# A fused attention and mixture-of-experts layer on one core: the weight-splitting steps at other places of a timetable

## The chip, the cores and the metric

The kernel runs on one core of a Trainium2 chip. The metric is the device time of one execution in microseconds; the time of a kernel is the median of its runs. The engines are TensorE (PE in the rows, PEld for its weight loads), VectorE (DVE), ScalarE (ACT), GpSimd (POOL) and SyncE (SP), which only issues DMAs. Each engine works through its own instructions in order, and waits on semaphores at the head of its queue.

## The reference

Eight sequences of 512 tokens with 256 features go through a pre-norm attention layer with 16 causal heads, then through a pre-norm layer of 8 experts, of which each token uses the 2 with the highest gate probability.

```python
x = x + attention(layernorm(x), W_qkv, b_qkv, W_out, b_out)      # 16 heads of 16, causal softmax
# second part, E = 8, H = 1024, TOP_K = 2
xn = (x' - mu) * rsqrt(var + 1e-5) * gamma + beta                 # x' = layernorm(x)
probs = softmax(xn @ gate_w); w, idx = top_k(probs, 2); w = w / w.sum()
h = gelu(einsum('bld,edh->eblh', xn, w1) + b1)                    # exact gelu
out_e = einsum('eblh,ehd->ebld', h, w2) + b2
x = x + sum over the two chosen experts of w * out_e + x'
```

## The kernel before

The program has three stages in the time of the core. First the projections of q, k and v (to 121 us). Then the attention, in 32 units (`UNITS`) of one batch and four heads each, which ends at about 508 us. Last the experts' matrix products over gathered tiles of 256 or 128 tokens, from 518 us on.

**The timetable.** From the attention on, nothing in the code says directly in which order an engine works. A table `table_of` maps a tick, a plain integer, to steps; `at(tick, stage, n)` adds one. Sorted by tick (and within a tick by the order in which the steps were added) it is one list, and every engine runs through it and does the part of each step that belongs to it. A tick is no time: it only orders. One unit has `UNIT = 48` ticks, so unit u lies from 48u on, and four units (192 ticks) are a batch.

**Per unit.** Five `combo` steps at 48u + 2, 11, 20, 30, 39: PE makes the transposed scores of unit u (L658) into three PSUM banks in turn, and the plain scores of a unit that comes 11 slots later (L630, L643); ACT takes the exponentials (L907, and L904 in the fifth combo), which frees the banks; DVE takes the row maxima of the later scores (L1240, L1242 with L1243, L1237). `load_unit` u + 3 at 48u - 4 makes SP issue eight DMAs with the q and k of a later unit (L1816, L1818); it waits until PE has made all scores of unit u - 1. `copy_o` (L927) copies the weighed values out. `keep_o`, `move_o`, `keep_inverse`, `move_inverse` (L1835, L1846, L1848, L1855, L1864) are SP's transfers of the results of earlier units through memory.

**Per batch.** The output projection and the second norm: `out_proj` and `gate` on PE (L716, L717 and L733), `load_again` on SP (L1890, the batch's x once more), `add_out` on DVE (L1260, which waits for it), `gamma` and `beta` on GpSimd for batches below 6 (L1756, L1759), `row_high` on ACT (L950), which waits for SP's `acc_out` (L1986) to have landed, and `rows_out` (L1978).

**Splitting the experts' weights.** The experts' products run in float16, with each weight as a high and a low part. 32 pieces of 128x1024 values (`W_SPLITS`) are split during the attention. Piece i takes these steps, in which `raw` is the piece in float32:

- `load_raw` i on SP (L1874), a DMA of 512 KB into the buffer for raw pieces. It waits until the piece that was in this buffer before has been split (`w_low`).
- `high_weights` i on ACT (L980): the float16 high part.
- `low_weights` i on DVE (L1402): the rest, from the raw piece and the high part. It waits for the high part.
- `store_weights` i on SP (L1882), for the first six pieces (`LENT = 6`) only. Their place in SBUF is still lent to the attention, so both parts are stored to memory with two DMAs and come back after it.

The first six pieces use one raw buffer and one pair of buffers for the parts:

```python
# load_raw, i < 6: the raw buffer of the piece before
w.wait_ge(sem("w_low"), raw_before[i] + 1)
# high_weights on ACT and low_weights on DVE, 0 < i < 6: all stores so far have landed
w.wait_ge(sem("w_stored"), 32 * i)
# store_weights
w.wait_ge(sem("w_low"), i + 1)
```

Pieces 6 to 31 use two raw buffers in turn, and write straight to the weights' place.

In the text behind this, high(i), low(i), raw(i) and store(i) are these four steps of piece i, and (u, c) is combo c of unit u.

Of the kernel before, what the change touches and what calls it, by code (L numbers as in the profile page):

```python
# [61 lines left out]
def build(nc, t):  # L62
# [54 lines left out]
    with ctx:  # L117
# [80 lines left out]
        LENT = -(-(HG * PT_LEN + V_LEN) // HALF)  # L198
# [87 lines left out]
        W_SPLITS = len(splits)  # L286
# [16 lines left out]
        UNIT = 48  # L303
# [13 lines left out]
        def at(tick, stage, n):  # L317
            table_of.setdefault(tick, []).append((stage, n))

        for u in range(UNITS):  # L320
            base = u * UNIT
# [39 lines left out]
        at(8 * 36 + 94, "spread_tops", 0)  # L361
        at(8 * 36 + 126, "find_scales_2", 0)

        split_ticks = [426 + UNIT * i for i in range(LENT)]
        split_ticks += [718 + 26 * i for i in range(W_SPLITS - LENT)]
        for i, base in enumerate(split_ticks):
            at(base - (24 if i < LENT else 35), "load_raw", i)
            at(base, "high_weights", i)
            at(base + 9, "low_weights", i)
            if i < LENT:  # L370
                at(base + 15, "store_weights", i)
# [7 lines left out]
        for b in range(B):  # L379
            base = (b + 1) * NG * UNIT  # L380
# [45 lines left out]
        for i, (batches, _, _, _) in enumerate(PARTS):  # L426

            base = max(ranked_at[batches - 1] + 16, 7 * NG * UNIT + 88) + (168 if i > ALL else 0)
# [11 lines left out]
        for j in range(-1, TILES):  # L440
            base = over + 58 + TILE_TICKS * j
# [1577 lines left out]
```

## Time and profile before

| | |
|---|---|
| median of 3 runs | 939.74 us |
| lowest, highest | 935.47, 952.23 us |
| the profiled execution: its own time | 935.47 us |
| its span, first to last instruction | 933.7 us |
| PE busy | 828.8 us, 89% of the span |
| DVE, ACT, POOL busy | 697.3, 572.1, 466.5 us |
| mean granted TensorE clock | 0.945 |

The profiled execution is the fastest of the three runs. Its time is 1.8 us longer than its span. The busy time of a stage is to be read beside the length of the stage: PE is nearly full in the experts' stage, and shares the attention with DVE and ACT.

### The profile page before, as it was taken

To read this page: it belongs to the slowest core of one execution; us is meant where nothing else is said; L and a number is where in the kernel's file an instruction comes from. 1 tells how busy PE (TensorE), PEld (TensorE's weight loads), DVE (VectorE), ACT (ScalarE), POOL (GpSimd) and SP (SyncE) were. 2 spreads that over 40 slices of the span, in tenths; PEclk is the share of its full clock that TensorE was granted. 3 is DMA by queue.
4 is the path that set the end of the run, shared out by engine and by line. 5 is a ranking of instruction groups with operands and counts; after the bars stand their busy time and mean duration, and the time that the engine had idled before them with its cause. 6 is when DMAs were issued, how large, how long until landed. Compare 5 with 4: busy or idle time off the path is not lost.

```text
span 933.7 us, 21008 instructions
## 1 busy us (share of the span) xinstructions
PE 828.8 (89%) x6760; PEld 551.7 (59%) x6760; DVE 697.3 (75%) x1566; ACT 572.1 (61%) x1048; POOL 466.5 (50%) x575
## 2 busy tenths in 40 slices
PE   4899988887888879887977799989999999999996
PEld 3555522332433324342424698868888888888875
DVE  6777889778689897979795587866676756666654
ACT  1867566657868787978686474544544444454543
POOL 4100023333635847767577548783577555455432
PEclk9999988889999988898899799999999999999999
DMA  9888758755777676577827884453436453444341
GB/s 210 257 281 269 250 174 239 207 130 172 230 199 221 185 196 183 166 212 183 218 75 248 151 140 78 78 116 65 81 62 92 74 82 70 84 72 80 49 70 24
DMA packets 185047, 139.40 MB, mean 149 GB/s; under 512 B 98064, under 2 KB 167568, under 8 KB 184816
## 3 DMA queue, kind: packets, MB, share of 16 engines
q1 hardware_dynamic: 153444, 95.16, 39.8%
q0 software_dynamic: 15776, 18.95, 13.0%
q10 hardware_dynamic: 15724, 23.95, 7.9%
q8 instruction: 61, 1.00, 0.5%
q14 instruction: 42, 0.34, 0.1%
HBM read 83.63 MB, written 44.80 MB: 138 GB/s over the span
## 4 chain that ended last, share of the span: by engine, by line
PE 54%; DVE 16%; DMA 13%; SPq 6%; issue 4%; POOL 3%; ACT 3%; POOLq 0%; ACTq 0%
PE banks L777 18%; PE banks L795 17%; PE banks L599 5%; DMA arena<-qk_parts 3%; DVE arena L1240 3%; PE banks L716 3%; PE banks L702 2%; PE banks L589 2%; DVE weights L1402 2%; PE banks L658 2%; DVE arena L1242 2%; DMA out<-arena 2%; DMA arena<-arena 2%; DMA arena<-token_rows,arena 2%; SPq L1816 2%
## 5 line engine op out<-in xcount | busy, mean ns | idle before, releaser
L996 ACT ACTIVATE arena<-banks,arena 128x256 f32<-128x256 f32 (+1 forms) x312 | 152.8, 542 | 188.8 <-PE banks L777 98.0
L777 PE MATMUL banks<-arena,weights 128*128 128x256 f16 (+1 forms) x1872 | 207.8, 268 | 12.7 <-DMA arena<-arena 11.9
L777 PEld LDWEIGHTS banks<-arena,weights 128*128 x1872 | 175.8, 99 | 39.4 <-issue 14.6
L795 PE MATMUL banks<-weights,arena 128*128 x1704 | 193.9, 273 | 0.8 <-DVE arena L1532 0.7
L1739 POOL DMA_INDIRECT out<-arena x71 | 115.0, 1620 | 145.5 <-DVE arena L1543 98.5
L795 PEld LDWEIGHTS banks<-weights,arena 128*128 128x128 f16 x1704 | 165.2, 98 | 22.4 <-issue 1.7
L658 PE MATMUL banks<-arena 64*128 64x128 f16 (+3 forms) x512 | 119.4, 326 | 17.8 <-ACT arena L907 5.5
L1530 DVE TENSOR_SCALAR arena<-arena 128x512 f16<-128x512 f32 (+1 forms) x156 | 75.2, 482 | 77.9 <-ACT arena L996 76.1
L630 PE MATMUL banks<-arena 62*128 62x384 f16 (+3 forms) x512 | 92.7, 324 | 32.6 <-DVE arena L1237 9.0
L1532 DVE SCALAR_TENSOR_TENSOR arena<-arena 128x512 f16<-128x512 f32 (+1 forms) x156 | 110.2, 706 | 5.6
L658 PEld LDWEIGHTS banks<-arena 64*128 64x128 f16 x512 | 38.4, 99 | 99.0 <-ACT weights L907 26.3
L1240 DVE TENSOR_REDUCE arena<-banks 128x2 f32<-128x1024 f32 x64 | 77.9, 1217 | 20.5 <-PE banks L643 20.0
L907 ACT ACTIVATE arena<-banks,arena 128x512 f32<-128x512 f32 x128 | 81.8, 686 | 18.3 <-PE banks L658 17.6
L907 ACT ACTIVATE weights<-banks,arena 128x512 f32<-128x512 f32 x128 | 80.3, 684 | 11.1 <-PE banks L658 10.6
L1715 POOL DMA_INDIRECT arena<-token_rows,arena x71 | 76.2, 1073 | 20.2 <-issue 18.0
L1686 POOL DMA_INDIRECT slot_tokens<-arena x64 | 68.0, 1062 | 21.6 <-issue 17.0
L1242 DVE TENSOR_REDUCE arena<-banks 128x2 f32<-128x768 f32 x64 | 60.9, 951 | 20.5 <-PE banks L643 20.2
L1700 POOL TENSOR_SCALAR_AFFINE_SELECT weights<-weights 128x512 f32<-128x512 f32 (+1 forms) x80 | 45.0, 580 | 60.2 <-ACT weights L907 55.3
L1700 POOL TENSOR_SCALAR_AFFINE_SELECT arena<-arena 128x512 f32<-128x512 f32 (+1 forms) x80 | 47.5, 610 | 39.4 <-ACT arena L907 37.8
L1543 DVE SCALAR_TENSOR_TENSOR arena<-banks,arena 128x256 f32<-128x256 f32 x71 | 31.4, 480 | 44.6 <-PE banks L795 41.4
L702 PE MATMUL banks<-arena 128*32 128x256 f32 (+3 forms) x512 | 57.1, 525 | 6.1 <-ACT arena L927 2.3
L630 PEld LDWEIGHTS banks<-arena 62*128 62x128 f16 x512 | 28.7, 98 | 54.8 <-DVE arena L1237 13.3
(199 smaller groups left out, 1273.9 us busy)
## 6 DMA issues: line engine op xcount, KB each, us to landing
weights<-in_L_ffn_w ACTq DMA_DIRECT2D x16, 1024.0 KB, 8.8
arena<-in_L_ffn_w SPq DMA_DIRECT2D x32, 512.0 KB
qk_parts<-weights SPq DMA_DIRECT2D x64, 128.0 KB
arena<-qk_parts SPq DMA_DIRECT2D x128, 64.0 KB, 3.4
weighed_values<-arena SPq DMA_DIRECT2D x32, 256.0 KB
token_rows<-arena SPq DMA_DIRECT2D x12, 512.0 KB, 4.3
arena<-qk_parts SPq DMA_DIRECT2D x128, 32.0 KB, 3.5
arena<-weighed_values SPq DMA_DIRECT2D x32, 128.0 KB
```

The costliest lines, as they stand in the source:

```text
L630: pe.matmul(bank[:, to:to + (qt + 1) * P], q_st[u % 4][half, h, qt * P:qt * P + P], k_st[u % 4][half, h, 0:(qt + 1) * P], start=(to == 0), ...
L658: m = pe.matmul(turn_bank(number)[:, to:to + T - kt * P], k_st[u % 4][half, h, kt * P:kt * P + P], q_st[u % 4][half, h, kt * P:T], start=T ...
L777: m = pe.matmul(bank[:, c * TILE:c * TILE + WIDTH[j]], w1[:, k, wp, f:f + P], xp[:, k, 0:WIDTH[j]], start=(i == 0), stop=(i == len(terms) ...
L795: m = pe.matmul(bank[:, c * D:(c + 1) * D], hp[:, f, c * P:(c + 1) * P], w2[:, f // (FC // 2), wp, f % (FC // 2), :], start=(f == 0 and i ...
L907: act.activation(p_T[u % 2][:, PAIR * h + j, PT_AT[kt]:PT_AT[kt] + T], bank, ACT.Exp, scale=EXP_SCALE).then_inc(sem("exped"), 1)
L996: m = act.activation(h_32[r % 2][:, c, 0:WIDTH[j]], banks[:, 1 + c2, c * TILE:c * TILE + WIDTH[j]], ACT.Gelu, bias=b1_now[j % 2][:, 2 * c2 ...
L1240: m = v.tensor_reduce(out[:, :, slot // 2, 3], pair, AX.X, ALU.max, negate=True)
L1242: v.tensor_reduce(out[:, :, slot // 2, 2], pair[:, :, 0:3 * P], AX.X, ALU.max, negate=True)
L1532: v.scalar_tensor_tensor(h_low[:, pair, width], h_32[r % 2][:, :, width], SCALE_H, h_high[:, pair, width], ALU.mult, ALU.subtract).then_in ...
L1700: m = g.affine_select(out=area, in_=area, compare_op=ALU.is_ge, fill=0.0, base=0, pattern=pattern, channel_multiplier=-1)
L1715: g.indirect_dma_start(gathered[j % 3][:, c, :], None, rows_dram[:, :], bass.IndirectOffsetOnAxis(slot_of(j, c), 0)).then_inc(sem(f"gather ...
L1739: g.indirect_dma_start(acc_dram[:, :], bass.IndirectOffsetOnAxis(slot_of(j, c), 0), y[j % 2][:, c, :], None, compute_op=ALU.add).then_inc( ...
```

## The change

Two numbers of the timetable are changed for the first six pieces, and one for the others. The steps of piece i < 6 stand 42 ticks apart and no longer 48, from the same first tick. Their `load_raw` stands 30 ticks ahead of `high_weights` and no longer 24. Pieces 6 to 31 stand 24 ticks earlier, with the same distance of 26 ticks.

```diff
-        split_ticks = [426 + UNIT * i for i in range(LENT)]
-        split_ticks += [718 + 26 * i for i in range(W_SPLITS - LENT)]
+        split_ticks = [426 + 42 * i for i in range(LENT)]
+        split_ticks += [694 + 26 * i for i in range(W_SPLITS - LENT)]
         for i, base in enumerate(split_ticks):
-            at(base - (24 if i < LENT else 35), "load_raw", i)
+            at(base - (30 if i < LENT else 35), "load_raw", i)
             at(base, "high_weights", i)
             at(base + 9, "low_weights", i)
             if i < LENT:
                 at(base + 15, "store_weights", i)
```

The instructions of PE and POOL keep their order. Those of ACT, DVE and SP change places.

On ACT, in unit 11 (L932 is a copy of the batch's turned rows, L960 and L966 copies of the output projection and the gate). Before:

```order
L907 ACTIVATE arena<-banks,arena 128x512 x2
L932 COPY arena<-banks 128x512
L907 ACTIVATE arena<-banks,arena 128x512 x4
L904 ACTIVATE arena<-banks,arena 128x2x256 x2
L927 COPY arena<-banks 128x512
L980 ACTIVATE arena<-arena 128x1024
L960 COPY arena<-banks 128x512
L966 COPY arena<-banks 128x32
```

Now:

```order
L907 ACTIVATE arena<-banks,arena 128x512 x2
L932 COPY arena<-banks 128x512
L907 ACTIVATE arena<-banks,arena 128x512 x2
L980 ACTIVATE arena<-arena 128x1024
L907 ACTIVATE arena<-banks,arena 128x512 x2
L904 ACTIVATE arena<-banks,arena 128x2x256 x2
L927 COPY arena<-banks 128x512
L960 COPY arena<-banks 128x512
```

high(3) moved from behind the copy that ends the unit to a place between the exponentials of (11, 2) and of (11, 3).

On SP, around the eight loads of unit 14, of which the last stands first here. Before:

```order
L1818 DMA arena<-qk_parts 16x2x512
L1835 DMA weighed_values<-arena 128x512
L1864 DMA arena<-inverse_sums 64x1x512
L1827 DMA arena<-v_rows 128x4x64
L1882 DMA late_weights<-arena 128x1024 x2
L1855 DMA inverse_sums<-arena 128x16
L1920 DMA arena<-arena 2x8x128 x2
L1874 DMA arena<-in_L_ffn_w 128x4x256
```

Now, from the row ahead of the eight loads on (six of them are left out):

```order
L1848 DMA arena<-weighed_values 128x1x16
L1986 DMA out<-arena 128x4x256
L1874 DMA arena<-in_L_ffn_w 128x4x256
L1816 DMA arena<-qk_parts 32x2x512
...
L1818 DMA arena<-qk_parts 16x2x512
L1882 DMA late_weights<-arena 128x1024 x2
L1835 DMA weighed_values<-arena 128x512
```

raw(3) moved from behind the eight loads to the place ahead of them, where it waits for low(2), and store(2) now follows them at once.

On SP, at `load_again` of batch 4. Before:

```order
L1978 DMA token_rows<-arena 128x4x256
L1874 DMA arena<-in_L_ffn_w 128x1024
L1846 DMA arena<-weighed_values 64x1x512
L1848 DMA arena<-weighed_values 128x1x16
L1890 DMA arena<-in_L_attn_x 128x4x256
```

Now:

```order
L1978 DMA token_rows<-arena 128x4x256
L1846 DMA arena<-weighed_values 64x1x512
L1848 DMA arena<-weighed_values 128x1x16
L1890 DMA arena<-in_L_attn_x 128x4x256
L1874 DMA arena<-in_L_ffn_w 128x4x256
```

The load of a raw piece moved from ahead of `load_again` to behind it.

## Rows read from the trace of the kernel before

**Rows 1.** Busy by stretch: length, PE, PEld, DVE, ACT, POOL, PEclk, DMA share, GB/s

```profile
212.00:256.00 44.00, 35.97 (x305) 15.54 (x301) 35.00 (x65) 34.70 (x60) 24.12 (x37) 0.92 0.67 207
256.00:300.00 44.00, 37.43 (x324) 15.57 (x321) 38.67 (x80) 35.60 (x64) 18.51 (x29) 0.92 0.73 204
300.00:475.00 175.00, 148.97 (x1209) 68.21 (x1207) 151.54 (x281) 139.04 (x238) 118.67 (x158) 0.90 0.70 189
```

**Rows 2.** The 26 later high parts by source line: durations, first and last start

```profile
L980 ACT ACTIVATE weights<-arena x26: 1130/1147/1171, 291.8 to 469.6; 128x1024 f16<-128x1024 f32 x26
```

**Rows 3.** Timeline of DVE, in unit 10

```profile
242.02 1.23 DVE L1240 TENSOR_REDUCE arena<-banks 128x2 f32<-128x1024 f32 x1
```

**Rows 4.** The low parts of the first six pieces by source line

```profile
L1402 DVE SCALAR_TENSOR_TENSOR arena<-arena x6: 1276/1277/2209, 223.9 to 283.1; 128x1024 f16<-128x1024 f32 x6
```

**Rows 5.** Timeline of SP's queue, units 10 and 11

```profile
241.81 0.33 SPq L1816 DMA_DIRECT2D arena<-qk_parts  x1
...
244.99 0.43 SPq L1818 DMA_DIRECT2D arena<-qk_parts  x1
...
247.57 0.98 SPq L1882 DMA_DIRECT2D late_weights<-arena  x2
...
250.60 0.40 SPq L1874 DMA_DIRECT2D arena<-in_L_ffn_w  x1
```

**Rows 6.** The stores of the first six pieces, issue to landing

```profile
DMA to landing us min/median/max: 2.0/3.2/4.5
```

**Rows 7.** Timeline of ACT, unit 11: start, length, idle time before

```profile
248.58 1.24 ACT L907 ACTIVATE arena<-banks,arena 128x512 f32<-128x512 f32 x2
250.15 1.27 ACT L907 ACTIVATE arena<-banks,arena 128x512 f32<-128x512 f32 x2 [0.32 <-PE banks L658]
...
254.68 1.15 ACT L980 ACTIVATE arena<-arena 128x1024 f16<-128x1024 f32 x1 [1.32 <-DMA arena<-in_L_ffn_w]
```

**Rows 8.** Timeline of PE, from the last combo of unit 11

```profile
251.43 0.38 PE L658 MATMUL banks<-arena 64*128 64x256 f16 x2
...
251.86 1.08 PE L716 MATMUL banks<-arena 128*128 128x256 f32 x4
...
253.87 1.85 PE L733 MATMUL banks<-arena 128*128 128x8 f32 x16
```

**Rows 9.** Chain of waits, 205 to 300 us: start, length, what

```profile
283.18 2.13 DVE arena L1402
285.33 0.33 SPq L1882
...
295.44 5.36 DMA arena<-qk_parts
```

**Rows 10.** Timeline of GpSimd, 336 to 341 us

```profile
336.79 2.36 POOL L1759 TENSOR_TENSOR arena<-arena 128x1024 f32<-128x1024 f32 x1
```

**Rows 11.** Timeline of DVE, the same stretch

```profile
335.90 1.16 DVE L1240 TENSOR_REDUCE arena<-banks 128x2 f32<-128x1024 f32 x1
336.98 3.25 DVE L1402 SCALAR_TENSOR_TENSOR weights<-arena,weights 128x1024 f16<-128x1024 f32 x1
```

**Rows 12.** Chain of waits, 390 to 436 us

```profile
403.83 1.67 SPq L1874
...
406.76 8.14 DMA arena<-in_L_attn_x
...
414.92 0.69 DVE arena L1260
```

**Rows 13.** Chain of waits, 440 to 520 us, the end of the attention

```profile
473.35 1.19 DVE weights L1402
...
492.59 5.74 DMA arena<-inverse_sums
...
510.70 7.45 DMA arena<-arena
```

**Rows 14.** Timeline of DVE: the first step that needs all low parts

```profile
484.76 0.16 DVE L1419 TENSOR_SCALAR arena<-arena 128x8 f32<-128x8 f16 x1
```

## The prediction

> **What bounds the kernel now.** I first read the busy time by stretch, since the change lies between 212 and 475 us only. In the long stretch from 300 to 475 us, 175 us, PE is busy for 149.0, DVE for 151.5 and ACT for 139.0 [rows 1]. No engine is the bound alone: each is at 79 to 87%, and each waits for the next in turn. PE cannot start a score before ACT has freed a bank, ACT cannot take exponentials before PE has made the score, and DVE's maxima free the banks of the plain scores. From 212 to 300 us PE is at 82 and 85%, DVE at 80 and 88% [rows 1]. So work that is moved within this part is neither free nor paid in full. What counts is whether it stands on the chain at its place. The number of steps is the same in both kernels, 32 high and 32 low parts.
>
> For a tick's size I take the high parts of pieces 6 to 31. Between ticks 718 and 1368 they start from 291.8 to 469.6 us [rows 2]: 177.8 us for 650 ticks, 0.274 us each.
>
> **The change part by part.** The last 26 pieces stand 24 ticks earlier and 26 apart. So piece i + 1 stands now 2 ticks behind the place that piece i had. Nearly the whole train of steps keeps its surroundings with the number shifted by one. What is left is this: one piece more is split before tick 728, none is split at 1368 to 1377, and some steps jump over a neighbour that stands within 2 ticks. The first six need a look each. I find five places that move time.
>
> (a) The store of piece 2 lands late, a cost. raw(3) now stands at tick 522, ahead of the eight loads of unit 14, and waits for low(2) at 519. On DVE low(2) follows the maxima of (10, 4), which end at 242.02 + 1.23 = 243.25 [rows 3]; it takes 1.28 [rows 4], to 244.53. SP then issues raw(3) in 0.40 [rows 5], to 244.95 with the gap, and the eight loads, which took 244.99 + 0.43 - 241.81 = 3.61 [rows 5], to 248.56. Only then come the two stores of piece 2, 0.98 [rows 5], to 249.54, the second of them issued at about 249.05. A store lands 3.2 us after its issue, at least 2.0, at most 4.5 [rows 6]: at 252.25 (251.05 to 253.55). high(3) stands now right behind the exponentials of (11, 2), which end at 248.58 + 1.24 = 249.82 [rows 7], and waits for this landing: 2.4 us (1.2 to 3.7). ACT is in order, so the exponentials of (11, 3) stand behind it: high(3) takes 1.15 [rows 7], one exponential about 0.65 (half of 1.27 for two), and the bank that PE needs for the last score of (11, 4) is free at 252.25 + 1.15 + 0.65 = 254.05. PE made it at 251.43 [rows 8]. That is 2.6 later (1.4 to 3.9). PE goes from there through the output projection and the gate without a pause, to 253.87 + 1.85 = 255.72 [rows 8], and so passes the delay on in full. The old wait of high(3) for its raw piece, 1.32 [rows 7], gives nothing back, since PE was busy with that projection over it. The loads of unit 14 also go out 3.2 later (245.0 for 241.8), but their first use is the fifth combo of unit 11, which this same wait puts off. **+2.6 us (+1.4 to +3.9).**
>
> [...]
>
> (b) low(5) leaves the place where it collided, a gain. The chain of waits runs through low(5) from 283.18, 2.13 long, then through SP's store(5), and on to the loads of unit 18, whose landing PE awaits [rows 9]. It is the one of the first six that took 2.21 where the others took 1.28 [rows 4]. Now it stands 30 ticks earlier, and low(6) comes in at tick 703, ahead of the same loads: 2.13 out and 1.28 in, with SP's raw(8) waiting for it as store(5) did. **-0.9 (-2.1 to 0;** the first end if low(6) falls into a wait for PE**).**
>
> (c) In batch 2 GpSimd's beta step, L1759, runs from 336.79 to 339.15 [rows 10]. A low part that starts at 336.98 takes 3.25 and not 1.28 [rows 11]: it does not run until GpSimd is done, and then takes its own time. The reduction ahead of it, which reads PSUM, took 1.16 with its head in the same stretch [rows 11]. The low part that now stands here, at tick 885 for 883, is behind the maxima of tick 884. These run while GpSimd does, and the low part ends at 340.2 as before. About 1.2 us of reductions, priced by the one in the row, are so taken out of DVE's queue, but the chain goes on by SP and a store from the low part's end, where the raw load of that tick has also fallen behind `acc_out`. I take two thirds. **-0.8 (-1.2 to 0).**
>
> (d) At `load_again` of batch 4 the chain has SP's raw load, 1.67 long, then the load of x, 8.14 to landing, then DVE's L1260 [rows 12]. The raw load stood at tick 1125 and stands at 1127, behind the load of x at 1126 (the order shows it). So x is asked for 1.67 us earlier. Of this DVE can take what it waited; the chain going through it says that it did wait. **-1.6 (-1.7 to 0).** If the two transfers of 512 KB shared the engines, x lands even sooner, but then DVE is held by something else at once, so I don't count it.
>
> (e) The last low part, on the chain at 473.35 with 1.19 [rows 13], is gone from there; its follower stands at tick 1353, where the batch's output projection keeps PE busy and DVE light. **-1.2 (-1.3 to 0).**
>
> The other pieces of the first six move 6 to 30 ticks within the same units; each ACT step of 1.15 and DVE step of 1.28 is paid as before, and I cost them at nothing, give or take 1 us.
>
> Sum: 2.6 - 0.9 - 0.8 - 1.6 - 1.2 = **-1.9 us**. The ends are +3.9 with no gain at all, and 1.4 - 2.1 - 1.2 - 1.7 - 1.3 = -4.9. The profiled execution took 935.47, so its like would take 933.6. It is the fastest of three runs, the median is 939.74; against that I forecast **937.8 us**.
>
> **The rivals.** *The queue holds, slower.* The mechanism is (a) alone: SP, with a load that waits for DVE ahead of work for PE. It decides if store(2) lands after 249.8 us, and its price is 2.6 to 3.9. The gains then come to nothing because each has a second wait right behind it, which the chain doesn't show. For it: three engines at 80 to 87% [rows 1], where a step taken off one often leaves the next at the same time. Against it: (d) and (e) remove time from the chain itself. It gives 939.7 + 2.6 = 942.3, up to 943.6.
>
> *The attention ends with the train, much earlier.* The split steps end 24 ticks earlier, 24 x 0.274 = 6.6 us; if the rest came after them, the time would be 933.1. Against it: the first step that needs all the low parts, L1419, runs at 484.76 [rows 14], 10 us behind the last of them at 473.35 + 1.19 = 474.5 [rows 13], and behind the attention the chain runs through transfers, 5.74 for the inverse sums and 7.45 for the turned tiles [rows 13], which the change doesn't touch.
>
> *Nothing moves.* The store lands in time, or PE's wait is covered, and the gains are covered too: PE's order is the same and the work is the same. It gives 939.7.
>
> **How the numbers follow.** The forecast, between -5 and -0.5 us, has 0.42; the slower rival 0.27; nothing moves 0.17; the early end 0.12; 0.02 are for what I don't see. The largest of these effects is under 1% of the time, so the chance of a change within 2%, which is about what a measurement of this kernel can tell from none, is 0.96; faster by more 0.015, slower by more 0.025. The range goes from the profiled run less all gains, 935.5 - 4.9 = 930.6, to the median with the whole cost, 943.6, and a little further up since one of three runs took 952.23: 930 to 945. It leaves out no case above, only runs that scatter.
>
> **What would show it.** (a): in unit 11 ACT waits 1.2 to 3.7 us before L980 for a landing of late_weights, and PE's L733 there starts some 2.6 later, counted from unit 10. (b): no L1402 of the first six above 1.3 us, and unit 18's loads issued sooner. (c): a low part beside L1759 of batch 2 with under 2.5 us, behind an L1242. (d): L1890 of batch 4 ahead of the raw load, and DVE's wait before L1260 under 0.5. (e): the last L1402 runs beside the output projection of batch 5, and L1419 starts sooner behind it. I am wrong if ACT finds the store landed, if a low part falls into one of GpSimd's other long steps, or if a longer pause of PE lowers its granted clock for some microseconds.

## The result, and the profile after

| | before | changed |
|---|---|---|
| median of 16 runs | 940.72 us | 950.52 us |
| lowest, highest | 935.47, 952.23 us | 939.97, 966.98 us |
| profiled execution, span | 933.7 us | 943.5 us |
| ratio of the times, 95% interval | | 1.0074 [1.0044, 1.0104] |

The change makes the kernel slower by 0.74%, some 7 us. That is less than 2%, but clear of no change. The ratios leave out the runs in which the chip was disturbed, so this one is smaller than that of the two medians; the profiled executions of experiments 3 and 11 are such runs.

The loss has a place. From PE's trace I took the start of every unit, the first L658 of its first combo. Unit 11, between the starts of (11, 0) and (12, 0), took 12.78 us before (242.87 to 255.65) and takes 20.75 now (245.59 to 266.34). In the profiled execution that is 8.0 of the 9.8 us. One us of it is only a matter of where I start to count, since the step ahead, from (10, 4) to (11, 0), got 1.0 shorter: from (10, 4) to (12, 0) it was 14.5 us and is 21.5, 7.0 more. Elsewhere the two executions drift apart and together again. The changed kernel was already 2.7 us behind at the start of unit 9, of which 1.7 at the start of unit 8, ahead of the first step that moved. It was 10.7 behind at unit 12, 16.6 at unit 26, 12.5 at unit 31 and 9.8 at the end. So one pair of executions does not prove the place; the experiments have to.

SP's queue in unit 11 after the change; start and length of each issue:

```profile
248.14 0.39 SPq L1874 DMA_DIRECT2D arena<-in_L_ffn_w  x1
248.64 0.44 SPq L1816 DMA_DIRECT2D arena<-qk_parts  x1
249.12 1.48 SPq L1818 DMA_DIRECT2D arena<-qk_parts  x1
...
252.98 0.43 SPq L1818 DMA_DIRECT2D arena<-qk_parts  x1
253.45 0.90 SPq L1882 DMA_DIRECT2D late_weights<-arena  x2
254.45 0.40 SPq L1835 DMA_DIRECT2D weighed_values<-arena  x1
254.89 0.53 SPq L1864 DMA_DIRECT2D arena<-inverse_sums  x1
```

It answers to [rows 5]. raw(3), L1874, stands ahead of the loads of unit 14 and goes out at 248.14, when low(2) is done. The chain of waits has the two side by side:

```profile
246.84 1.29 DVE arena L1402
...
248.14 0.39 SPq L1874
```

The eight loads follow, one of them 1.48 long, and the stores at 253.45. What my prediction never named is the last row. L1864 is `move_inverse` of unit 7, the transfer of the inverse softmax sums of batch 1's last group.

Two rows of the kernel before, SP's issue of this transfer and GpSimd's step that waits for it:

```profile
245.93 0.53 SPq L1864 DMA_DIRECT2D arena<-inverse_sums  x1
...
250.33 1.27 POOL L1677 TENSOR_TENSOR arena<-arena 128x512 f32<-128x512 f32 x1 [0.41 <-DMA arena<-inverse_sums]
```

Counted from the start of (10, 4) on PE, 241.15 before and 244.83 after, the transfer went out at 4.8 and goes out at 10.1; L1677 started at 9.2 and starts at 14.5. The rest of the way is the chain of waits of the changed kernel:

```profile
254.89 4.17 DMA arena<-inverse_sums
...
259.28 1.27 POOL arena L1677
...
260.60 2.07 PE banks L716 x4
```

L716 is the output projection of batch 1, which needs the divided values. Now the timelines of ACT and PE in the changed kernel, with the idle time ahead in brackets:

```profile
256.41 1.15 ACT L980 ACTIVATE arena<-arena 128x1024 f16<-128x1024 f32 x1 [3.53 <-DMA late_weights<-arena]
```

```profile
258.19 0.60 PE L658 MATMUL banks<-arena 64*128 64x256 f16 x2 [2.98 <-ACT arena L907]
...
260.60 2.07 PE L716 MATMUL banks<-arena 128*128 128x256 f32 x4 [1.48 <-POOL arena L1677]
262.68 1.91 PE L716 MATMUL banks<-arena 128*128 128x256 f32 x4
264.56 1.85 PE L733 MATMUL banks<-arena 128*128 128x8 f32 x16
```

They answer to [rows 7, 8]. Two waits stand behind one another: 3.53 us of ACT for the store of piece 2, which comes to 2.98 on PE, and 1.48 of PE for L1677. Only the last of them to end decides when L716 starts. And then the first group of L716 took 1.08 before [rows 8] and takes 2.07. The stretch from the start of the output projection to the next unit's scores, before and after, with PE's granted clock behind the counts:

```profile
251.86:255.65 3.79, 3.79 (x29) 3.38 (x28) 1.29 (x2) 2.47 (x4) 1.97 (x6) 1.00 0.90 282
```

```profile
260.60:266.34 5.74, 5.74 (x26) 4.63 (x27) 0.00 (x0) 0.00 (x0) 2.18 (x6) 0.66 0.84 220
```

PE is busy the whole time in both, but at a mean granted clock of 1.00 before and 0.66 after: behind the pauses, most of this stretch is granted the lower of the two levels, 1.2 and not 2.4 GHz. From L716 to (12, 0) it was 14.5 - 10.7 = 3.8 us and is 21.5 - 15.8 = 5.7. So the 7.0 us are 5.1 for the later start of L716 and 1.9 for the clock.

### The profile page after: what moved, and what is told of

It is laid out like the page before. It is cut to its first block, busy times and chain, and to the rows that moved or that the text cites. A ratio compares the mean times of both kernels' runs of the same rounds, so it can differ in the third digit from the quotient of the medians.

```text
span 943.5 us, 21008 instructions
## 1 busy us (share of the span) xinstructions
PE 835.8 (89%) x6760; PEld 553.9 (59%) x6760; DVE 697.6 (74%) x1566; ACT 572.8 (61%) x1048; POOL 465.0 (49%) x575
## 4 chain that ended last, share of the span: by engine, by line
PE 52%; DVE 17%; DMA 14%; SPq 7%; issue 4%; POOL 2%; ACT 1%; POOLq 0%; ACTq 0%; DVEq 0%
PE banks L777 17%; PE banks L795 17%; PE banks L599 5%; DVE arena L1240 3%; PE banks L716 3%; DMA arena<-inverse_sums 2%; DMA weighed_values<-arena 2%; SPq L1818 2%; PE banks L702 2%; DVE weights L1402 2%; PE banks L589 2%; SPq L1816 2%; DVE arena L1242 2%; DMA arena<-token_rows,arena 2%; DVE arena L1237 2%
## 5 line engine op out<-in xcount | busy, mean ns | idle before, releaser
L777 PE MATMUL banks<-arena,weights 128*128 128x256 f16 (+1 forms) x1872 | 205.3, 266 | 12.3 <-DMA arena<-arena 11.7
L795 PEld LDWEIGHTS banks<-weights,arena 128*128 128x128 f16 x1704 | 165.2, 98 | 22.3 <-issue 1.7
L658 PE MATMUL banks<-arena 64*128 64x128 f16 (+3 forms) x512 | 121.4, 334 | 19.4 <-ACT arena L907 6.9
L630 PE MATMUL banks<-arena 62*128 62x384 f16 (+3 forms) x512 | 95.7, 330 | 34.3 <-DVE arena L1237 11.6
L658 PEld LDWEIGHTS banks<-arena 64*128 64x128 f16 x512 | 38.4, 100 | 105.4 <-issue 34.4
L1240 DVE TENSOR_REDUCE arena<-banks 128x2 f32<-128x1024 f32 x64 | 77.9, 1217 | 21.2 <-PE banks L643 20.8
L907 ACT ACTIVATE arena<-banks,arena 128x512 f32<-128x512 f32 x128 | 81.2, 687 | 12.9 <-PE banks L658 12.2
L1686 POOL DMA_INDIRECT slot_tokens<-arena x64 | 68.2, 1066 | 23.3 <-issue 16.5
```

The lines of the kernel that those rows point to most:

```text
L630: pe.matmul(bank[:, to:to + (qt + 1) * P], q_st[u % 4][half, h, qt * P:qt * P + P], k_st[u % 4][half, h, 0:(qt + 1) * P], start=(to == 0), ...
L658: m = pe.matmul(turn_bank(number)[:, to:to + T - kt * P], k_st[u % 4][half, h, kt * P:kt * P + P], q_st[u % 4][half, h, kt * P:T], start=T ...
L777: m = pe.matmul(bank[:, c * TILE:c * TILE + WIDTH[j]], w1[:, k, wp, f:f + P], xp[:, k, 0:WIDTH[j]], start=(i == 0), stop=(i == len(terms) ...
L795: m = pe.matmul(bank[:, c * D:(c + 1) * D], hp[:, f, c * P:(c + 1) * P], w2[:, f // (FC // 2), wp, f % (FC // 2), :], start=(f == 0 and i ...
L907: act.activation(p_T[u % 2][:, PAIR * h + j, PT_AT[kt]:PT_AT[kt] + T], bank, ACT.Exp, scale=EXP_SCALE).then_inc(sem("exped"), 1)
L1240: m = v.tensor_reduce(out[:, :, slot // 2, 3], pair, AX.X, ALU.max, negate=True)
```

## The experiments

The theories. **Theory I** (inverse sums): SP's wait for low(2) ahead of unit 14's loads holds the whole queue, and the loss ends in `move_inverse` of unit 7, by L1677 and the output projection. **Theory S** (store): the loss is ACT's wait for store(2), my term (a). **Theory P** (phase): it is spread over the 26 later pieces and their new neighbours. Theory Q is I and S together, the loss at raw(3). Each figure is a ratio to the kernel before on the same chip with its 95% interval; the chips of the experiments ran the kernel before in medians of 966 to 970 us, so ratios are compared and not times. In the table all times are in us; the columns after the second are of the one profiled execution: unit 11's length, then, from the start of (10, 4), SP's issue of L1864, the start of L1677, the first L716, and the start of (12, 0).

| kernel | ratio | unit 11 | L1864 | L1677 | L716 | (12, 0) |
|---|---|---|---|---|---|---|
| before | 1 | 12.8 | 4.8 | 9.2 | 10.7 | 14.5 |
| changed | 1.0074 [1.0044, 1.0104] | 20.8 | 10.1 | 14.5 | 15.8 | 21.5 |
| changed, again | 1.0091 [1.0060, 1.0122] | 22.3 | 9.8 | 14.3 | 15.9 | 23.3 |
| 1 first six alone | 1.0067 [1.0029, 1.0104] | 22.7 | 9.8 | 14.6 | 16.1 | 23.5 |
| 2 rest two ticks later | 0.9966 [0.9931, 1.0001] | 13.7 | 4.8 | 9.1 | 10.7 | 14.5 |
| 3 raw(3) behind loads | 1.0062 [1.0026, 1.0098] | 18.9 | 7.1 | 12.9 | 14.2 | 19.7 |
| 4 store(2) ahead | 1.0086 [1.0049, 1.0123] | 22.4 | 10.3 | 14.5 | 15.8 | 23.2 |
| 5 inverse 7 ahead | 1.0026 [0.9995, 1.0057] | 18.2 | -0.2 | 8.0 | 13.8 | 19.0 |
| 6 before, raw(3) ahead | 1.0087 [1.0057, 1.0116] | 20.8 | 9.9 | 14.3 | 15.6 | 21.5 |
| 9 before, inverse 7 late | 1.0072 [1.0039, 1.0104] | 20.5 | 8.8 | 14.1 | 15.5 | 21.3 |
| 11 both ahead | 1.0003 [0.9952, 1.0053] | 18.0 | 1.0 | 8.4 | 13.4 | 18.8 |
| 12 as 2, inverse 7 ahead | 0.9968 [0.9936, 1.0001] | 13.7 | -0.6 | 8.7 | 10.7 | 14.5 |
| 13 as 2, again | 0.9964 [0.9928, 0.9999] | 13.6 | 4.8 | 8.8 | 10.7 | 14.5 |

The last column says where the loss is. What it stands above 14.5, as a share of the kernel's time, is 0.74% and 0.91% for the changed kernel, 0.92, 0.53, 0.90, 0.46, 0.73, 0.70 and 0.45% for experiments 1, 3, 4, 5, 6, 9 and 11, and nothing for 2. Each of these lies within the interval of its ratio. So this one stretch is enough to account for every loss measured here.

**1. Where: the first six pieces.** The change without the shift of pieces 6 to 31:

```diff
-        split_ticks += [694 + 26 * i for i in range(W_SPLITS - LENT)]
+        split_ticks += [718 + 26 * i for i in range(W_SPLITS - LENT)]
```

> The change for the first six pieces alone (42 ticks apart, raw load 30 ahead), the other 26 stay at 718. Theory Q, that the loss sits at raw(3) in SP's queue in unit 11, expects the whole loss here: 0.6 to 0.9% slower than before, and unit 11 some 6 to 8 us longer. Theory P, that the loss is spread over the 26 later pieces and their new neighbours, expects at most 0.2% slower here.

0.67% slower, and unit 11 at 22.7 us is 9.9 longer, above the 6 to 8 expected. The loss is in the first six, and theory P, which allowed 0.2%, falls.

**2. The later pieces' new neighbours.** The kernel before, with one number:

```diff
-        split_ticks += [718 + 26 * i for i in range(W_SPLITS - LENT)]
+        split_ticks += [720 + 26 * i for i in range(W_SPLITS - LENT)]
```

> The kernel before with pieces 6 to 31 two ticks later (720 for 718): the same neighbours as in the changed kernel, such as load_again of batch 4 ahead of the raw load, without the extra piece at 694 and with the first six untouched. My prediction's terms (c) and (d) expect 2.4 us less, -0.25%. Theory P expects a loss of 0.3 to 0.7%. Theory Q expects no change within 0.3%.

It is 0.34% faster, near the 0.25% of my terms (c) and (d); by its interval alone that could be nothing. The loss of 0.3 to 0.7% that theory P expected is ruled out.

**3 and 4. Which step of SP.** Both start from the changed kernel:

```diff
-            at(base - (30 if i < LENT else 35), "load_raw", i)
+            at(524 if i == 3 else base - (30 if i < LENT else 35), "load_raw", i)
```

> The changed kernel with one step moved by two ticks: raw(3) at 524, behind the eight loads of unit 14 and no longer ahead of them. Theory Q expects most of the loss gone: 0 to 0.3% slower than before, ACT's wait before high(3) under 1 us, the inverse sums of unit 7 asked for some 4 us sooner, unit 11 no more than 2 us longer than before. Theory P expects 0.6 to 0.8% slower still.

```diff
-                at(base + 15, "store_weights", i)
+                at(523 if i == 2 else base + 15, "store_weights", i)
```

> The changed kernel with store(2) at tick 523, right behind raw(3) and ahead of the eight loads of unit 14. If the loss in unit 11 is ACT's wait for the store (3.5 us in the changed kernel), that wait goes and 3 us or more of the 8 come back. If it is the transfer of the inverse sums of unit 7, which stands behind all of these in SP's queue, nothing comes back: that transfer goes out no sooner, GpSimd's L1677 and PE's output projection start as late, and the time stays 0.6 to 0.8% above before.

Experiment 3 missed what theory Q expected. With raw(3) behind the loads these start as early as before, but raw(3) and store(2) are still ahead of L1864 and wait for low(2): it goes out at 7.1, and unit 11 loses 6.1 us for 8.0. ACT's wait was 1.25 us. Of the two cases in the expectation of experiment 4 the second came: nothing is won. ACT still waited 2.57 us, since the store took longer to land, and L716 starts at 15.8 as in the changed kernel. PE in experiment 4, in (11, 4) and at the output projection:

```profile
258.80 0.39 PE L630 MATMUL banks<-arena 62*128 62x512 f16 x2 [2.23 <-DMA arena<-qk_parts]
...
262.28 2.08 PE L716 MATMUL banks<-arena 128*128 128x256 f32 x4 [2.52 <-POOL arena L1677]
```

PE's wait of 2.98 for ACT is gone, but two others have taken its place. One is 2.23 us for the loads of unit 14, which go out behind the stores here, 1.0 us later than in the changed kernel. The other is L1677, 2.52 for 1.48. In the changed kernel's second profile PE waited 1.45 us for these loads too, so they are a third transfer that the held queue makes late.

**5. The transfer of the inverse sums ahead.** The changed kernel with

```diff
-            at(after + returns[3], "move_inverse", u)
+            at(521 if u == 7 else after + returns[3], "move_inverse", u)
```

> The changed kernel with one step of SP moved: the transfer of unit 7's inverse sums (L1864) goes ahead of raw(3) and so ahead of SP's wait for low(2). Theory I, that the loss in unit 11 ends in this transfer, expects GpSimd's L1677 at about 9 us behind the start of (10, 4) and no longer at 14.5. ACT's wait of 3.5 us for store(2) is then the last: PE's output projection starts at about 14.0 for 15.8, unit 11 takes 18 to 19 us for 20.8, and the time is 0.4 to 0.6% above before. Theory S, that ACT's wait for the store is the whole cause, expects unit 11 unchanged at 20 to 21 us.

L1677 starts at 8.0 without a wait, L716 at 13.8 and unit 11 takes 18.2 us, as theory I had it. The time is 0.26% above before, less than the 0.4 to 0.6% expected. ACT's wait of 3.42 us is left, and it is now the last:

```profile
260.71 0.59 PE L658 MATMUL banks<-arena 64*128 64x256 f16 x2 [2.92 <-ACT arena L907]
...
261.42 2.02 PE L716 MATMUL banks<-arena 128*128 128x256 f32 x4
```

**9. The transfer late, and nothing else.** The kernel before, in which no split step moves:

```diff
-            at(after + returns[3], "move_inverse", u)
+            at(546 if u == 7 else after + returns[3], "move_inverse", u)
```

> The kernel before with this transfer alone moved, from tick 534 to 546: it goes out about 4.7 us later, and nothing of the split steps is touched. Theory I expects L1677 at about 14 us behind (10, 4) for 9.2, the output projection some 4 us late, and with PE's clock lowered by the pause 5 to 7 us more in unit 11: 0.5 to 0.7% slower than before. Theory S expects no change.

This is the decisive one. One DMA, asked for 4 us later, makes the kernel 0.72% slower, as much as the whole change. GpSimd and PE in this run:

```profile
259.46 1.26 POOL L1677 TENSOR_TENSOR arena<-arena 128x512 f32<-128x512 f32 x1 [5.37 <-DMA arena<-inverse_sums]
```

```profile
260.77 2.07 PE L716 MATMUL banks<-arena 128*128 128x256 f32 x4 [4.58 <-POOL arena L1677]
```

PE waits 4.58 us, and its first projection then takes 2.07 as after the change. Unit 11 is 7.7 us longer, a little above the 5 to 7 expected.

**11. The edits of 4 and 5 together.**

> The changed kernel with both waits mended: store(2) at 523 behind raw(3), and unit 7's inverse sums at 521. Theory I with S expects the output projection at 11 to 13 us behind (10, 4), unit 11 at 13 to 16 us, and a time within 0.3% of before or under it. What is left above before would have to come from the loads of unit 14, which go out 4 us later here than before.

1.0003, but the interval is the widest here, up to 1.0053, and holds experiment 5's 1.0026 too. It does not show that the loss is gone. Unit 11 still takes 18.0 us, more than expected, and from (10, 4) to (12, 0) it is 4.3 us above before, 0.45%, which the interval allows. What is left is what the expectation named, the loads of unit 14:

```profile
258.74 0.39 PE L630 MATMUL banks<-arena 62*128 62x512 f16 x2 [2.20 <-DMA arena<-qk_parts]
```

Experiment 4 has the same wait with 2.23. ACT also waits 2.48 us for the store, and the exponential behind it ends about 0.2 us after PE has these loads, so that mending one of the two alone would probably win little.

**The changed kernel again**, beside 5, 9 and 11.

> The changed kernel once more, beside the others on this chip. Every theory expects 0.7% slower than before, 0.5 to 0.9, and unit 11 at 20 to 22 us.

0.91% slower and unit 11 at 22.3 us, just above both ranges. The granted clock costs more here: from L716 to (12, 0) it is 7.4 us at a mean clock of 0.50, for 5.7 at 0.66 in the first profile.

**6. raw(3) alone.** The kernel before, with the one step of SP that the change puts ahead of the loads:

```diff
-            at(base - (24 if i < LENT else 35), "load_raw", i)
+            at(522 if i == 3 else base - (24 if i < LENT else 35), "load_raw", i)
```

> The kernel before with raw(3) alone moved from tick 546 to 522, ahead of the eight loads of unit 14. It waits there for low(2), which ends 5.3 us behind the start of (10, 4), where SP in before started the loads at 0.65. Theory I, by SP's queue, expects the inverse sums of unit 7 at about 10.5 for 4.8, L1677 at 14 to 15, unit 11 at 18 to 21 us for 12.8, and the time 0.5 to 0.9% above before, although no step of ACT or DVE has moved. If the places on ACT and DVE matter and SP's queue does not, no change.

0.87% slower, unit 11 at 20.8 us, L1864 at 9.9. ACT, DVE, PE and GpSimd have the order of the kernel before. So SP's order alone does it: a DMA moved 24 ticks forward in its queue, to where its own wait holds the rest. ACT's wait for the store is not ahead of PE's scores here, and L716 still starts at 15.6, in experiment 9 at 15.5, where the changed kernel has 15.8. So in the changed kernel the wait for the store adds next to nothing to that of the inverse sums: the two overlap, and the later one counts. Only with the transfer out of the way, in experiment 5, does the store decide, and L716 starts at 13.8.

**12 and 13. The later pieces again.** 12 is experiment 2 with the edit of 5, 13 is experiment 2 once more.

> Pieces 6 to 31 two ticks later as in the second kernel here, which came out at 0.9966, and the inverse sums of unit 7 at tick 521 for 534. In before that transfer had let L1677 end 0.2 us ahead of PE's need, so it should add little: 0.2 to 0.6% faster than before, within 0.1% of the kernel without it.

> The kernel with pieces 6 to 31 two ticks later, once more, to see if its 0.34% holds on another set of runs. My terms (c) and (d) expect 0.2 to 0.5% faster; if the first figure was scatter, within 0.15% of before.

The three kernels with pieces 6 to 31 two ticks later came out at 0.9966, 0.9968 and 0.9964. Each interval reaches about 1, and 12 and 13 share their runs of the kernel before, but three of one sign make a gain of 0.3% likely. Moving the transfer of unit 7 further ahead adds nothing, as expected: before, L1677 ended in time for PE.

One wait goes with the new places in nearly all profiles: ACT's ahead of `row_high` (L950) of batch 2, for `acc_out`. Before, and in experiment 13:

```profile
346.93 1.04 ACT L950 CAST arena<-arena 128x1024 f16<-128x1024 f32 x1 [1.85 <-DMA out<-arena]
```

```profile
349.88 1.09 ACT L950 CAST arena<-arena 128x1024 f16<-128x1024 f32 x1
```

The raw load of tick 891, now 893, no longer stands ahead of this batch's `acc_out` at 892. In the four kernels with the old place (before, 1, 6, 9) this wait is 1.6 to 1.9 us. Of the nine profiles with the new place it is nothing in eight, and 1.35 in experiment 4. That it is this wait that makes the 0.3% is not shown: the changed kernel has lost it too.

## Why the prediction was wrong

I forecast 937.8 us, in 930 to 945, and a gain of 0.2%; it is a loss of 0.74% and 950.5 us. The slower rival had the sign and the mechanism, "SP, with a load that waits for DVE ahead of work for PE", but at 942 to 944 us not the size.

**(a) is the step that failed,** by its size and by the transfer that sets it: +2.6 us (+1.4 to +3.9) forecast, 7.0 measured from (10, 4), where its sum begins, to (12, 0). The sign named for it, L733 some 2.6 us later counted from unit 10, came out at 7.0 as well. The first half was right. raw(3) waits for low(2), the loads follow, then the stores, and high(3) waited 3.53 us for a landing, where I had 2.4 (1.2 to 3.7). The second half stopped one row too early. I named what the held queue does to store(2) and to unit 14's loads, and did not go on down the queue. `move_inverse` of unit 7 stands two rows below the stores in the order of the changed kernel. Before, its result was ready 0.3 us ahead of PE (L1677 to 10.45, L716 at 10.71), so there was no slack. Experiment 9 shows that this transfer alone, late by 4 us, costs as much as the whole change. Experiment 5 shows what is left without it: the store's wait and the clock behind it, 4.5 us up to (12, 0) and 0.26% of the time. I also took PE's run from (11, 4) through the output projection at its old length. After the pauses it took 5.7 us for 3.8 from L716 on, at the lower clock (7.4 in the second profile). I had named that only as something that could go wrong, and gave it no price.

**(b), no gain, and a loss in its place.** low(5) no longer collides. The row of the changed kernel that answers to [rows 4], with the longest of the first six at 1.28 and not 2.21:

```profile
L1402 DVE SCALAR_TENSOR_TENSOR arena<-arena x6: 1275/1278/1284, 226.2 to 286.3; 128x1024 f16<-128x1024 f32 x6
```

But GpSimd's L1756 of batch 1 holds DVE all the same, with another instruction. The three small ones in this row took 2.71 us together:

```profile
292.17 2.71 DVE L1079 SCALAR_TENSOR_TENSOR arena<-arena 128x32 f32<-128x32 f32 x3
```

So the collision was passed on. And the sign that I named, unit 18's loads issued sooner, came out the other way: counted from the start of (14, 4) they go out at 4.8 us in the changed kernel and at 4.4 in its second profile, where it was 2.4. From (12, 0) to (16, 0) the changed kernel took 51.7 and 50.8 us, for 49.7 before and 48.9 to 49.2 in experiments 2, 6, 9 and 13. I have not taken apart which neighbour does this.

**(c), right at its place, then moved.** Beside L1759 of batch 2 there is no long low part any more, which is better than I had it. But one now stands beside L1759 of batch 3, where none did:

```profile
403.86 2.37 POOL L1759 TENSOR_TENSOR arena<-arena 128x1024 f32<-128x1024 f32 x1
```

```profile
404.39 2.92 DVE L1402 SCALAR_TENSOR_TENSOR weights<-arena,weights 128x1024 f16<-128x1024 f32 x1
```

In the second profile of the changed kernel the low part started first, and L1759 took 3.34 us instead. I looked for collisions that go, and not for those that come.

**(d), smaller than I had it.** `load_again` of batch 4 does stand ahead of the raw load, and DVE's wait ahead of L1260 there was still 0.78 us where I had set a bound of 0.5. Before, that wait was 1.64, so 0.9 us of the 1.6 went. In total L1260 waited 3.7 us in the changed kernel and 3.8 before, since in batch 2 it waited 2.3 for 0.6.

**(c) with (d), and `acc_out`.** Their sum without the first six is what experiments 2 and 13 time: -0.34 and -0.36% for -0.25%. That the sum is near is in part luck: there too a low part stands beside L1759 of batch 3, with 2.89 us, so (c) is not the gain that I had. In the changed kernel itself I can't see it: with the shift it stands at 1.0074 and 1.0091, without it, experiment 1, at 1.0067.

**(e), not to be told.** L1419 runs at 497.19, 12.4 us later than before [rows 14], with the unit starts around it. Units 28 and 29 were 2.3 and 1.0 us shorter than before in the profiled execution, but one execution scatters by as much.

The rival of an early end is refuted by the time, and "nothing moves" by experiments 1, 6 and 9.

What stays open: which neighbours hold up unit 18's loads, and which of the later pieces' makes the 0.3%.

## What to carry to other kernels

When a step with a wait moves forward in an in-order DMA queue, go down the queue behind it until every step has been checked against the moment at which its reader needs it, not only the first two. Look above all for the one whose result arrives just in time in the kernel before. One small transfer held for 4 us cost as much here as the whole change, since the pause on PE is followed by a stretch at the lower clock.

The waits that a held queue causes can overlap. Taking one of them away shows what it is worth only if it was the last to end: moving the store won nothing, moving the inverse sums did.

A count of collisions that vanish is no gain until the new order has been searched for those that appear.

## What the runs showed of the hardware

The stores took longer to land when their places in the queue changed. The twelve stores took 2.0 to 4.5 us, median 3.2, before [rows 6]. In the changed kernel:

```profile
DMA to landing us min/median/max: 2.2/4.3/7.0
```

Issued right ahead of eight loads rather than behind them, in experiment 4, store(2) did not free ACT as I expected: issued 4.9 us sooner, it cut ACT's wait from 3.5 to 2.6 us only. high(3) started 6.7 us behind the issue of the second of the two stores, where it was 2.5 in the changed kernel.

A pause of PE ahead of the output projection is followed by the lower granted clock. In the four profiles without one (before, 2, 12, 13) the first four matmuls of L716 took 1.08 us, and L716 to (12, 0) 3.8. In the nine with pauses of 2.2 to 4.8 us in all, in the last combo and ahead of L716, they took 1.95 to 2.08, and the stretch 5.2 to 7.4.

GpSimd and DVE hold each other up, and small instructions as much as large ones. In the changed kernel a group of three L1079 on 32 values each, 0.49 us elsewhere in the trace of before, took 2.71 beside L1756. The Trainium skill states such a lock, in "SBUF — State Buffer", section on the two separate sides: a DVE instruction with two inputs in SBUF and one of GpSimd that reads SBUF exclude each other, and the one that starts first has the ports for its whole length. The traces agree: in the collisions of L1756 and L1759 with a low part, before and after the change, GpSimd had started first and kept its 2.35 to 2.37 us, and the low part ended 1.1 us behind it. The other way round GpSimd waits: its L1677 that started inside low(1) before took 2.03 us, where 1.27 is usual.
